# A graph network's message layer: edge weights of two tiles in one product of 128 rows and 512 columns

## The reference, cut to what matters

```python
# layer 0: degree-normalised sum of neighbours' rows, added to x, layer norm
# layer 1, per edge e from src to dst; x1 is the layer-0 output, 12500 nodes x 32 = s (8) and v (8 x 3)
h = relu(edge_feat @ W1 + b1)                      # 212500 x 32 @ 32 x 64
w = (h @ W2 + b2).reshape(e, 4, 8, 8)              # 64 x 256: four 8x8 matrices per edge
m0 = ALPHA * (einsum('ei,eio->eo', s[src] * sh0, w_000) + C110 * einsum('eim,em,eio->eo', v[src], sh1, w_110))
m1 = ALPHA * (einsum('ei,em,eio->eom', s[src], sh1, w_011) + einsum('eim,eio->eom', v[src] * sh0, w_101))
out = segment_sum([m0, m1], dst) + self-interaction
x = layernorm(x1 + out)
```

## Time and profile before

| | us |
|---|---|
| median of three runs | 5195.7 |
| profiled execution: its span, first to last instruction | 5099.5 |
| median less span | 96.2 |
| layer 0 and set-up (in the span) | 0 to 1950 |
| message layer | 1950 to 5080 |
| end | 5080 to 5099.5 |

### The profile page before, as it was taken

The page is one execution under the profiler, slowest core; times in us unless marked ns, Lnnn a source line. Parts: engine busy times, 40 slices in busy tenths (PEclk is TensorE's granted clock), DMA queues, the critical chain, the costliest instruction groups (busy, mean ns, idle before and its releaser), DMA issues.

```text
span 5099.5 us, 54067 instructions
## 1 busy us (share of the span) xinstructions
PE 2903.2 (57%) x20030; PEld 2114.7 (41%) x20030; DVE 2791.7 (55%) x4344; ACT 1398.2 (27%) x1651; POOL 2381.5 (47%) x2475
## 2 busy tenths in 40 slices
PE   5566666666666664545545465455554555555555
PEld 3344444445444453333433343343333333333344
DVE  7444544445444534555655566556655655665566
ACT  3454555455545551111111111111111111111111
POOL 2444444453444335554455545545554554555453
PEclk7787878787878877677776677767767767777777
DMA  2000000000000010000000001100010110011011
GB/s 50 9 8 9 9 8 8 9 9 8 8 9 9 10 22 17 19 19 18 20 19 19 19 17 21 19 18 19 19 21 15 22 19 17 19 19 22 17 19 26
DMA packets 187965, 84.72 MB, mean 17 GB/s; under 512 B 131337, under 2 KB 174153, under 8 KB 187721
## 3 DMA queue, kind: packets, MB, share of 16 engines
q0 software_dynamic: 78336, 40.26, 5.4%
q1 hardware_dynamic: 109385, 41.08, 3.6%
HBM read 76.34 MB, written 4.81 MB: 16 GB/s over the span
## 4 chain that ended last, share of the span: by engine, by line
PE 30%; DVE 25%; issue 24%; another core or an unknown queue 14%; ACT 4%; DVEq 1%; DMA 1%; POOL 0%; SPq 0%; POOLq 0%; ACTq 0%
DVE stage L1404 10%; PE ps L767 9%; PE ps L881 8%; PE ps L724 6%; DVE prod_all L1394 5%; PE ps L782 5%; ACT room L572 4%; DVE prod_all L1388 3%; DVE oh L1108 2%; PE ps L873 1%; PE ps L755 1%; DVE prod_all L1220 1%; DVE stage L1413 1%; DVE sumT_all L1127 1%
## 5 line engine op out<-in xcount | busy, mean ns | idle before, releaser
L522 POOL DMA_INDIRECT xg<-x_table,idx x1664 | 1569.6, 943 | 1637.9 <-DVE stage L1378 1045.9
L881 PE MATMUL ps<-w2t,hT 128*128 128x256 f32 x3328 | 1037.4, 451 | 617.5 <-issue 403.6
L522 POOL DMA_INDIRECT xg<-scaled_x_table,idx x784 | 803.4, 1025 | 1007.8 <-issue 587.8
L881 PEld LDWEIGHTS ps<-w2t,hT 128*128 128x128 f32 x3328 | 736.8, 226 | 1019.0 <-issue 781.5
L572 ACT ACTIVATE room<-ps 128x1089 bf16<-128x1089 f32 x800 | 908.5, 1188 | 853.6 <-remote 495.6
L1388 DVE TENSOR_TENSOR prod_all<-ps,stage 128x768 f32<-128x768 f32 x416 | 397.7, 956 | 1245.4 <-remote 660.7
L767 PE MATMUL ps<-prod_all,lane 128*128 128x363 bf16 x2640 | 636.8, 355 | 577.5 <-issue 181.6
L724 PE MATMUL ps<-oh,stage 128*64 128x76 f32 x3328 | 378.0, 275 | 796.9 <-issue 561.7
L627 ACT ACTIVATE hT<-ps,b 64x512 f32<-64x512 f32 x416 | 284.1, 683 | 1764.0 <-remote 739.0
L1404 DVE TENSOR_REDUCE stage<-prod_all 128x192 f32<-128x1536 f32 x416 | 723.6, 1741 | 0.0
L724 PEld LDWEIGHTS ps<-oh,stage 128*64 128x64 f32 x3328 | 329.4, 175 | 819.7 <-issue 551.4
(11 more groups left out here) (141 smaller groups left out, 1312.5 us busy)
## 6 DMA issues: line engine op xcount, KB each, us to landing
efT<-in_efT SPq DMA_DIRECT2D x104, 256.0 KB
xg<-x_table,idx POOLq DMA_INDIRECT x1664
xg<-scaled_x_table,idx POOLq DMA_INDIRECT x784
sh<-in_sh SPq DMA_DIRECT2D x104, 32.0 KB
idx<-in_src SPq DMA_DIRECT2D x104, 8.0 KB
idx<-in_src SPq DMA_DIRECT2D x98, 4.0 KB
scaled_x_table<-room SPq DMA_DIRECT2D x2, 784.0 KB, 7.6
x_table<-x_sb SPq DMA_DIRECT2D x7, 224.0 KB, 4.3
```

What stands on the lines that cost most here:

```text
L522: pool.indirect_dma_start(rows[k][:, t, :], None, table, bass.IndirectOffsetOnAxis(ap=idx[k][:, t:t + 1], axis=0),).then_inc(s_g[layer][k] ...
L881: mm = pe.matmul(ps_w[j % 2][:, t, :], hT[j % 2][:, t * P:(t + 1) * P], w2t[:].rearrange("p c o i -> p (c o i)"), start=True, stop=True)
```

## The change

Two tiles share a product now. `w2t` becomes a block matrix of 128 x 512: rows 0 to 63 hold W2 in columns 0 to 255, rows 64 to 127 hold it in columns 256 to 511, the rest is zero. `hT` holds both groups of a pair on its 128 partitions, as they come out of the hidden product, so one rectification of 128 x 512 serves the pair, and one product of a 128-edge slice of `hT` with the block matrix gives the weights of a tile of the first group (columns 0 to 255) and of a tile of the second group (256 to 511). The bias can't be a row any more: it is added by a product in bfloat16 of a matrix of ones with `b2_parts`, whose rows 0, 32 and 64 hold the bias split into three bfloat16 parts; its 256 columns are read twice. A "group" for DVE is now two tiles of each of the pair's groups, and `slot_of` and `tile_of` translate between the order of the tiles in the input and their places. The harmonics are copied in two instructions of half the size, in that order. `hT` has a buffer for each pair.

```diff
-                for t in range(TPG):
-                    mm = pe.matmul(ps_w[j % 2][:, t, :], hT[j % 2][:, t * P:(t + 1) * P],
-                                   w2t[:].rearrange("p c o i -> p (c o i)"), start=True, stop=True)
+                for t in range(2):
+                    edges = slice((2 * (j % 2) + t) * P, (2 * (j % 2) + t + 1) * P)
+                    out = ps[:, 2 * (j % 2) + t, :]
+                    pe.matmul(out.rearrange("p (h n) -> p h n", h=2), ones_b[:],
+                              b2_parts[:].unsqueeze(1).to_broadcast([P, 2, WN]), start=True, stop=False)
+                    mm = pe.matmul(out, hT[j // 2][:, edges], w2_cols, start=False, stop=True)
                 mm.then_inc(s_w, 1)
...
-                if g >= 2:
-                    act.wait_ge(s_w, g - 1)
-                act.activation(hT[b][0:HID, :], ps_h[b], ACT.Relu, bias=b1[b * HID:(b + 1) * HID, :]).then_inc(s_relu, 1)
+                if pair >= 2:
+                    act.wait_ge(s_w, 2 * (pair - 1))
+                act.activation(hT[pair % 2][:], ps_h2, ACT.Relu, bias=b1[:]).then_inc(s_relu, 1)
...
-                act.activation(ps_sh[k], sh[k][:], ACT.Copy).then_inc(s_shp, 1)
+                for a in range(2):
+                    half = slice(8 * a, 8 * a + 8)
+                    act.activation(ps_sh[k][:, half].rearrange("p (t q) m -> p t q m", q=2),
+                                   sh[k][:, half].rearrange("p (q t) m -> p t q m", q=2), ACT.Copy).then_inc(s_shp, 1)
...
-                rectify(GPC * n)
-                rectify(GPC * n + 1)
+                rectify(2 * n)
                 scalars(n)
                 if n + 1 < CHUNKS:
                     harmonics(n + 1)
-                rectify(GPC * n + 2)
-                rectify(GPC * n + 3)
+                rectify(2 * n + 1)
...
-            for b in range(2):
-
-                pool.memset(hT[b][HID:P, :], 0.0).then_inc(s_hT1, 1)
-                pool.wait_ge(s_hT1, 2 * b + 1)
-                pool.memset(hT[b][HID:HID + 1, :], 1.0).then_inc(s_hT1, 1)
-                pool.wait_ge(s_hT1, 2 * b + 2)
+            pool.memset(w2_cols, 0.0).then_inc(s_wblank, 1)
+            pool.memset(ones_b[:], 1.0).then_inc(s_b2, 1)
+            pool.memset(b2_parts[:], 0.0).then_inc(s_b2, 1)
             pool.wait_ge(s_offsets, 4)
             pool.partition_all_reduce(spans[:], span[:], P, RMAX).then_inc(s_span, 1)
+
+            pool.wait_ge(s_b2in, 16)
+            pool.tensor_scalar(b2_row, b2_row, ALPHA, None, ALU.mult).then_inc(s_b2, 1)
...
+            for v in range(3):
+                pool.wait_ge(s_b2, 8 + 3 * v)
+                pool.tensor_copy(b2_part[v], b2_turned).then_inc(s_b2, 1)
+                pool.wait_ge(s_b2, 9 + 3 * v)
+                pool.tensor_copy(b2_parts[32 * v:32 * v + 1, :], b2_part[v][32 * v:32 * v + 1, :]).then_inc(s_b2, 1)
+                pool.wait_ge(s_b2, 10 + 3 * v)
+                pool.tensor_tensor(b2_turned, b2_turned, b2_part[v], ALU.subtract).then_inc(s_b2, 1)
...
-                        rows[k][:, t, :], None, table,
+                        rows[k][:, slot_of(t) if layer else t, :], None, table,
...
-            dve.tensor_copy(w2t[:, 0:2].rearrange("p c o i -> p c i o"), w2v[:, 1:3]).then_inc(s_w2x, 1)
-            dve.tensor_copy(w2t[:, 2:4].rearrange("p c o i -> p c i o"), w2v[:, 0:4:3]).then_inc(s_w2x, 1)
+            dve.wait_ge(s_wblank, 1)
+            for b in range(2):
+                half = slice(b * HID, (b + 1) * HID)
+                dve.tensor_copy(w2t[half, b, 0:2].rearrange("p c o i -> p c i o"), w2v[half, 1:3]).then_inc(s_w2x, 1)
+                dve.tensor_copy(w2t[half, b, 2:4].rearrange("p c o i -> p c i o"), w2v[half, 0:4:3]).then_inc(s_w2x, 1)
```

71 lines of the change are left out of this document (46 added, 25 removed).

## The result

The changed kernel takes 5114.5 us (5108.3 to 5125.2, four runs), the kernel before took 5199.8 us beside it: a ratio of 0.9841, 95% interval 0.9818 to 0.9864. That is faster by 1.6%, 85 us. I had forecast 5204 us, which is no change, with a range from 5121 to 5290. It moved where I had seen nothing to move it, and lies 6.5 us outside the range.

The account below looks back on a forecast made before the run. Waits bound the message layer, DVE being released only after POOL's two gathers. Span 5099.5 + 7 (products) + 0.6 (set-up) = 5107, plus 96.2 around it and the last chunk's slower group: some 5204 us, range 5121 to 5290.

Parts of the forecast that it names:

- the one on PE's instructions: PE in the message layer: 12 instead of 16 instructions a group, 120 instead of 136 a chunk; counted at nothing.
- the ring: Message layer, two chunks: release to features 12.2, POOL's start 1.4, two gathers 40.0, release 4.9; 58.5 us against 58.8 measured.
- tail: Message layer: time from the gathers' last DMA start to DVE's release, taken as 4.9 us of a pair of chunks.
- Rival A: PE's slow stretch is counted in instructions; fewer shorten the release by 1.6 us a pair: -83, 5121 us; chance 0.22.
- The mark that I set for A: Sign in the message layer that fewer PE instructions help: last DMA to release falls below 4 us.
- The 96.2 us around the span: Whole execution: median's excess over the profiled span, taken as launch and scatter and kept in the forecast.
- the slower cold group: PE's weights at half clock: 4.4 us against 3.5, +0.9 a group, covered by 2.0 us of the second gather.
- The warm group of 2.3 us: PE's weights at full clock: 2.34 us a group (2.20 to 2.74) against 1.97, +0.4.
- the rectification at nothing: ACT: 208 instructions of 0.683 us go, 142 us less work, none on the critical path; 0, bounds -10 and +10.
- The +7 us for the products after the release: PE's next weights after DVE's release: a third of pairs may lack cover, 17 x 0.4; bounds 0 and 47.
- Rival B: PE falls behind before the slow stretch, delaying group 1 in long chunks: +84 to +115, 5288 us, up to 5320; chance 0.31.
- Rival C: Message layer's slow stretch is an instruction fetch; 7 fewer at 22 us of wait: -150, 5050 us; chance 0.05.

## Why the prediction was wrong, point by point

**The step that failed** is the one on PE's instructions: "A group has 12 instead of 16 in the trace ... This matters where PE issues slowly, see the first rival". In the forecast it counted at nothing, because "PE's speed isn't in this sum while the weights are ready when DVE asks". But the ring as I wrote it held a term in which PE's speed stood: the 4.9 us from the last DMA to the release. Of the same pair I had noted that PE starts one MATMUL in about 1.4 us; such starts go on behind the last DMA of 3603.66:

```profile
3606.93 1.01 PE L873 MATMUL ps<-efT,w 128*128 128x512 f32 x1 [0.39 <-issue]
```

And the weights were not ready when DVE asked. In 37 of 47 pairs they end behind the last DMA's start, 6.8 us in the mean, and in most of them DVE follows at once. With fewer instructions they end ahead of it in 43 of 45. Measured: tail 6.85 to 5.93, pair 59.95 to 58.73. With the products doubled the tail is 7.17, and with PE not held neither change costs or gives anything.

**Rival A**, "fewer shorten it", had the direction and the cause of the gain, but not its size. It took all of the tail for a backlog of PE's instructions, with 1.6 us a pair and 83 us; measured were 0.9 from the tail, 1.2 a pair, 53 to 61 us in the layer. It had 0.22. Only what lies above some 5 to 6 us in the tail was PE's. The rest comes late whatever PE has done by then, as I had held against A ("however PE divides them"): with no bias product PE is through 15 us ahead of the last DMA, and the tail is 6.0 us. I had the sign of it in hand, for the prediction says "The completions come late too" (weights over at 3576.1, seen at 3590.1), but made no term of it. The mark that I set for A, a tail under 4 us, was wrong as well. I took 4.9 from one pair, where the mean is 6.85 (in both traces); it went to 5.93. By that mark A would have been rejected.

**The 96.2 us around the span** were a false constant: 1.9 us lie there. The layer's saving is a difference, so it isn't touched by this, but the forecast of rival A, 5121, took its level from it. The level came out right because the median that I had added them up to, 5195.7 us, is of three runs that the result's own before counts too. The forecast's own range was also added up loosely: its lower end, 5186, is 5195.7 less 10, its upper one 5204 and 30, while the terms' upper bounds come to 67.

**The ring's other terms** hold: two gathers without a gap, 39 us in the mean, 12.4 from the release to the features, 1.4 to the gather; the short chunk 19.2 us. My reading that the second gather covers the slower cold group is right too (short chunks 18.9 before, 19.2 after). The warm group of 2.3 us is right, the rectification at nothing is right (3054.0 against 3054.2 us), ACT's 151 us less came as reckoned and gave nothing. The +7 us for the products after the release did not show: that term went from 12.58 to 12.35.

**Rival B**, PE a group behind, had more chance than A and fell: no long chunk of the changed kernel has its long wait before group 1, where it was six of 47. I had worked with the +0.4 and +0.9 us of groups outside the held stretch, and set them beside a stretch in which a product takes 0.7 to 2.8 us whatever its columns. In that stretch fewer products weigh more than longer ones. Its converse showed in the doubled products: 12 such chunks, and slower.

**Rival C**, the instruction fetch: of the 47 held stretches of the changed kernel's first trace one has a fetch on that queue (q8) in it, of the 47 before three. The layer has 53 fetches where it had 59, about as C reckoned, but they don't lie where the time is lost.

The Trainium skill ("Perfetto Trace Analysis", DMA Instruction — SWDGE (GPSIMD)) says that the profiled end of such a DMA is when the descriptors are written, not when the data has moved. The traces agree: over the whole layer the first packet of a row DMA moves 1.65 us (median) behind the start of POOL's record of 0.94 us. They also show that no data piles up, for it is 1.65 us for the first DMA of a gather and for the sixteenth. Queues of the pair shown above, from 3542.6 to 3584 and from 3583.5 to 3597 us:

```profile
q0 software_dynamic: 1024, 0.53, 8.6%
...
DMA packets 0, 0.00 MB, mean 0 GB/s; under 512 B 0, under 2 KB 0, under 8 KB 0
```

The last of the 1024 packets of the 32 DMAs starts at 3583.4, 4 us ahead of the release.

## What stays open

What the engines share with the gathers is not settled. The runs show that it depends on the rate of the DMAs, that it sets in only after more than 10 us of them (eight DMAs hold nothing, sixteen alone do), that it ends behind the last DMA (5.1 to 6.0 us in the mean where the DMAs are 1.25 us apart and PE is through, 3.4 to 3.7 us in the three runs with a mean of 1.35), that what comes late is the report of finished work and, in part, PE's starts, and that the rows themselves are not late. A backlog of semaphore updates that builds up above one DMA in about 1.4 us, and has to drain, would look like this; no run measures its length, and why PE's starts come in steps of 0.7 us is open too. A kernel with fewer or larger descriptors for the same rows would tell, and wasn't tried.

A rival stands untested. Every execution on record has a span and a granted clock of its own, so each was recorded at least in part. Whether that recording takes part in the hold, no run here can say.

## What to carry to other kernels

When one engine starts its instructions singly and evenly, at steps that don't depend on their size, price what you add or take there by the instruction and not by its duration. Then ask of the term that ends the wait whether the engine's work or only the report of it is late: set the end of the product beside the start of the one that waits for it. If they are together, a shorter list helps; if they are microseconds apart, it doesn't. A mean over all such pairs is needed to see 1 us in 60; one pair's tail was 2 us off. And before such a stretch is tuned, try to break it up: a pause of 0.4 us in every second DMA of a gather, which makes POOL 16% slower, took 635 us from the layer (3054 to 2419), ten times what the change did.

## What the runs showed of the hardware

- 16 indirect DMAs of 128 rows at 1.25 us, twice in a row, hold PE: MATMULs start 1.4, 2.1 or 2.8 us apart, and DVE waits 20 us a pair. At 1.45 us apart it is mostly gone, and the kernel takes 0.852 of its time; at 1.55 and 1.70 it is 0.882 and 0.942, as POOL is then slower.
- In the same stretch finished work is reported late: DVE starts up to 22 us behind the end of the weights that it waits for (also with no slow MATMUL, in the run without bias products), ACT 17.5 us behind the hidden pair, and POOL 2.2 us behind its own write. The rows' packets move 1.65 us behind their DMA's start as ever.
- A POOL write of 8 columns between two of them is free outside a held stretch (0.12 us in a gap of 0.30); one of 512 columns costs 0.41 us net; four of 8 columns with waits 1.14.
- The same kernel takes 5100 to 5113 us on three chips and 5200 on another, so that a time from one can't be set against a trace from another to 2%.
